# Opening of an attention and FFN kernel: order of key splits, layer norm, query weights and first queries

## What is computed

```python
x = x + _L0_xattn_ref(_layernorm(x), ctx, ctx, proj_q, bias_q, proj_k, bias_k, proj_v, bias_v, w_out)
x = x + _L0_ffn_ref(_layernorm(x), w_gate, w_up, w_down)
...
q = jnp.einsum('bnd,hdk->bhnk', query, proj_q) + bias_q      # k and v in the same way, from ctx
attn = jax.nn.softmax(jnp.einsum('bhqk,bhnk->bhqn', q, k) / scale, axis=-1)
hid = heads of attn @ v;  result = hid @ w_out.T
...
h = silu(fp4_linear(x, w_gate)) * fp4_linear(x, w_up);  result = fp4_linear(h, w_down)
```

## Time and profile before

| | us |
|---|---|
| timed runs | 394.61, 397.33, 397.7 (median 397.33) |
| the profiled execution | 398.0, span 396.1 |
| PE busy | 333.8 (84% of the span) |
| DVE busy | 310.3 (78%) |
| ACT busy | 266.7 (67%) |
| POOL busy | 257.6 (65%) |

### The profile page before, as it was taken

How to read it: one execution, slowest core, us unless ns; L and a number is a source line. 1 busy time by engine, 2 the same in 40 slices (tenths; PEclk the granted TensorE clock), 3 DMA queues, 4 the chain that set the end, 5 groups by cost and what they waited for, 6 DMA issues and landing times.

```text
span 396.1 us, 9486 instructions
## 1 busy us (share of the span) xinstructions
PE 333.8 (84%) x3571; PEld 254.4 (64%) x3571; DVE 310.3 (78%) x629; ACT 266.7 (67%) x634; POOL 257.6 (65%) x254
## 2 busy tenths in 40 slices
PE   1777669998799989989895877898878999999976
PEld 1455448776587767767674666676656767677854
DVE  1979845766777778687899877679999999998692
ACT  3566687987899999999986689734352553542431
POOL 7272244786579898998985586738844667767510
PEclk9989958999999999999999899999998999999999
DMA  7990535797599899997995698831000000000001
GB/s 209 321 357 2 102 66 107 120 148 136 96 133 174 151 171 180 156 186 146 187 168 96 120 159 131 133 63 26 15 14 15 13 15 27 14 13 29 16 26 40
DMA packets 131710, 42.42 MB, mean 107 GB/s; under 512 B 123788, under 2 KB 129616, under 8 KB 131665
## 3 DMA queue, kind: packets, MB, share of 16 engines
q1 hardware_dynamic: 131665, 41.82, 55.3%
HBM read 8.78 MB, written 2.10 MB: 27 GB/s over the span
## 4 chain that ended last, share of the span: by engine, by line
DVE 42%; PE 32%; ACT 11%; issue 8%; POOL 4%; DMA 2%; SPq 0%; ACTq 0%; DVEq 0%
PE ps L572 5%; PE ps L493 5%; PE ps L495 5%; PE ps L494 5%; DVE arena L1191 4%; ACT arena L853 4%; DVE negmax L1110 4%; PE ps L629 4%; DVE arena L1141 3%; DVE arena L1193 3%; DVE arena L1314 3%; DVE arena L1280 2%; POOL arena L1387 2%; DVE arena L1126 2%; DVE arena L1145 2%
## 5 line engine op out<-in xcount | busy, mean ns | idle before, releaser
L1387 POOL TENSOR_TENSOR arena<-arena 128x640 f16<-128x640 f32 x64 | 93.0, 1453 | 58.0 <-ACT arena L863 57.6
L853 ACT ACTIVATE arena<-ps,negmax 128x154 f32<-128x154 f32 x256 | 78.6, 398 | 15.6 <-DVE negmax L1110 15.3
L572 PE MATMUL ps<-v_h,pT 128*128 128x132 f16 (+1 forms) x640 | 52.8, 214 | 17.2 <-DVE q_odd L1102 8.8
L1110 DVE TENSOR_REDUCE negmax<-ps 128x4 f32<-128x616 f32 x64 | 50.9, 795 | 20.1 <-PE ps L629 19.8
L572 PEld LDWEIGHTS ps<-v_h,pT 128*128 128x128 f16 x640 | 38.9, 100 | 24.6 <-issue 22.9
L1392 POOL TENSOR_TENSOR arena<-arena 128x256 f16<-128x256 f32 x64 | 46.5, 728 | 8.0 <-ACT arena L870 8.0
L863 ACT ACTIVATE arena<-arena 128x640 f16<-128x640 f32 x64 | 47.4, 741 | 1.2
L493 PE MATMUL ps<-arena 128*128 128x256 f16 (+1 forms) x144 | 41.6, 289 | 7.4 <-DVE arena L1013 5.9
L493 PE MATMUL ps<-arena,xnT_even 128*128 128x352 f16 x128 | 40.1, 313 | 4.8 <-DVE xnT_even L1202 4.1
L494 PE MATMUL ps<-arena 128*128 128x256 f16 (+1 forms) x144 | 41.3, 287 | 0.0
L495 PE MATMUL ps<-arena 128*128 128x256 f16 (+1 forms) x144 | 41.2, 286 | 0.0
(11 more groups left out here) (163 smaller groups left out, 943.7 us busy)
## 6 DMA issues: line engine op xcount, KB each, us to landing
out_dram<-arena SPq DMA_DIRECT2D x16, 128.0 KB, 1.7
pT<-arena SPq DMA_TRANSPOSE x70, 4.2
xs<-in_x_dram SPq DMA_DIRECT2D x2, 512.0 KB, 7.3
arena<-in_L_xattn_w_out_dram SPq DMA_DIRECT2D x1, 1024.0 KB, 11.8
xs<-in_x_dram SPq DMA_DIRECT2D x2, 384.0 KB, 6.7
wffn<-in_L_ffn_w_down_dram SPq DMA_DIRECT2D x1, 704.0 KB, 9.3
wffn<-in_L_ffn_w_gate_dram SPq DMA_DIRECT2D x1, 640.0 KB, 7.7
wffn<-in_L_ffn_w_up_dram SPq DMA_DIRECT2D x1, 640.0 KB, 8.2
```

The source lines that it names most:

```text
L572: last = pe.matmul(o[:, h0 * HB:h1 * HB], pT[:, n % RING_P, part * CHUNKS + c], v[:, b, j, at[0]:at[-1] + 1].rearrange("p m k -> p (m k)") ...
L853: last = act.activation(prob[:, j, k * LP:k * LP + L], ps[:, 2 * (j % 2) + k % 2, (k // 2) * L:(k // 2 + 1) * L], ACT.Exp, bias=negmax[:, ...
L1110: dve.tensor_reduce(negmax[:, s, 4 * j:4 * j + 4].rearrange("p (k u) -> p u k", k=2), v, AX.X, ALU.max, negate=True).then_inc(max_done, 1)
L1387: pool.tensor_tensor(part_of(j, 1), prob[:, j], part_of(j, 0), ALU.subtract).then_inc(p_low, 1)
```

## The change

- The first two loads of x bring the rows of steps 0 and 1, not of step 0 alone; proj_v is loaded ahead of the rest of x.
- PE does 12 transposes of the identity into a bank that nothing reads (`WARM`) behind those of ctx. Keys 0 to 2 are then computed first on chunk 0, then on chunk 1 of their inputs (`KEYS_FIRST`), each as soon as that chunk's weights are split (`wk_split`); keys 3 and 4 follow (`KEYS_NEXT`), then the turning of step 0's rows, keys 5 to 7, and the first two query tasks. The other two stand in slots 0 and 1.
- The low half of the key weights goes from DVE to POOL, ahead of the query weights'; bias_v's comes behind those.
- ACT splits the query weights ahead of all key copies, normalises step 1's rows ahead of slot 0, and splits the value weights behind the first two query copies.
- DVE runs one layer norm of 4 columns for steps 0 and 1 ahead of slot 0; statistics of steps 2 to 7 come in slots 0 to 2 and their layer norm (12 columns) in slots 3 and 4.
- Step 1's rows are turned in slot 0 (before: 5), its queries stand in slots 2 to 5 (6 to 9), values of batch 0 in slots 1 to 4 (0 to 3), output weights in slots 5 to 8 (4, 4, 5, 6), step 2's rows in slot 6 (5).

```diff
+WARM = 12
+KEYS_FIRST = 3
+KEYS_NEXT = 5
...
+        wk_split = sem("wk_split")
...
-            return n if b == 0 else 11 + 2 * n
+            return 1 + n if b == 0 else 11 + 2 * n
...
-            return (4, 4, 5, 6)[n]
+            return 5 + n
...
-            return 3 if i == 1 else 5 if i == 2 else 8 * (i - 1) - 6
+            return 6 if i == 2 else 8 * (i - 1) - 6
...
-            return 6 + p // 2 if i == 1 else 8 * (i - 1) + (2 if i == 2 else 1) + p
+            return p // 2 - 2 if i == 0 else 2 + p // 2 if i == 1 else 8 * (i - 1) + (2 if i == 2 else 1) + p
...
-            out = [t for i in range(1, STEPS) for t in query_tasks(i) if query_at(i, t[2]) == n]
-            out += [("x", 1)] if n == 5 else []
+            out = [t for i in range(STEPS) for t in query_tasks(i) if query_at(i, t[2]) == n]
+            out += [("x", 1)] if n == 0 else []
...
-        TASKS = [("x", 0)] + query_tasks(0)
+        FIRST_QUERIES = [t for t in query_tasks(0) if query_at(0, t[2]) < 0]
+        TASKS = [("x", 0)] + FIRST_QUERIES
...
+            def pairs_of_rows(b):
+                return x[b].rearrange("(i v p) d -> v p i d", v=2, p=P)
...
-                sp.dma_start(xs[:, v, 0], x[0, rows_of(0, v)]).then_inc(ld_x0, 16)
+                sp.dma_start(xs[:, v, 0:2], pairs_of_rows(0)[v, :, 0:2]).then_inc(ld_x0, 16)
...
+            load_proj("v", proj_v, ld_v)
...
-                pairs = x[b].rearrange("(i v p) d -> v p i d", v=2, p=P)
-                first = 1 if b == 0 else 0
+                first = 2 if b == 0 else 0
...
-                    sp.dma_start(xs[:, v, b * STEPS // B + first:(b + 1) * STEPS // B], pairs[v, :, first:]).then_inc(ld_x, 16)
-            load_proj("v", proj_v, ld_v)
+                    sp.dma_start(xs[:, v, b * STEPS // B + first:(b + 1) * STEPS // B],
+                                 pairs_of_rows(b)[v, :, first:]).then_inc(ld_x, 16)
...
+            for _ in range(WARM):
+                pe.transpose(ps[:, PROJ_BANK, 0:P], ident[:, :], ident[:, :])
+            def keys(p, c):
+                return three(bank(J_K + p)[:, 0:B * L], wk_h[:, c, p * P:(p + 1) * P], wk_l[:, c, p * P:(p + 1) * P],
+                             cT_h[:, c, :, 0:L], cT_l[:, c, :, 0:L], c == 0, c == KC - 1)
...
-            pe.wait_ge(w_low, 1)
-            for p in range(PAIRS):
+            for c in range(KC):
+                pe.wait_ge(wk_split, c + 1)
+                for p in range(KEYS_FIRST):
+                    if c == 0: free(J_K + p)
+                    last = keys(p, c)
+                    if c == KC - 1: last.then_inc(job_mm, 1)
+            def keys_of(p):
...
-                    last = three(bank(J_K + p)[:, 0:B * L], wk_h[:, c, p * P:(p + 1) * P],
-                                 wk_l[:, c, p * P:(p + 1) * P], cT_h[:, c, :, 0:L], cT_l[:, c, :, 0:L],
-                                 c == 0, c == KC - 1)
+                    last = keys(p, c)
...
-                        pe.wait_ge(w_low, 3)
+                        pe.wait_ge(w_low, 2)
...
+            for p in range(KEYS_FIRST, KEYS_NEXT):
+                keys_of(p)
...
-            pe.wait_ge(w_low, 2)
-            for t in query_tasks(0):
+            for p in range(KEYS_NEXT, PAIRS):
+                keys_of(p)
+            pe.wait_ge(w_low, 1)
+            for t in FIRST_QUERIES:
...
+            act.wait_ge(ld_q, 16)
+            split_proj("q", wq_h, 1.0)
...
-            for p in range(PAIRS):
+            for p in range(KEYS_NEXT):
...
-                if p == 3:
-                    act.wait_ge(ld_q, 16)
-                    split_proj("q", wq_h, 1.0)
...
+            for p in range(KEYS_NEXT, PAIRS):
+                keys_out(p)
...
-                if n == 3: act.wait_ge(ln_step, 2 * LN_ROWS)
-                for r in range(1, STEPS):
+                if n == rows_at(2): act.wait_ge(ln_step, 2 * LN_ROWS)
+                for r in range(2, STEPS):
...
-                        if r >= 2: rows_high(r)
+                        rows_high(r)
...
-            act.wait_ge(w_scaled, 1)
-            split_part("v", wv_h, 1.0, 0)
-            high(("q", 0, 0))
-            split_part("v", wv_h, 1.0, 1)
-            for t in query_tasks(0)[1:]:
+            act.wait_ge(ln_step, LN_ROWS)
+            rows_normal(1)
+            for t in FIRST_QUERIES:
...
+            act.wait_ge(w_scaled, 1)
+            split_proj("v", wv_h, 1.0)
...
-            dve.wait_ge(ld_k, 16)
-            for c in range(KC):
-                dve.wait_ge(w_high, c + 1)
-                last = dve.scalar_tensor_tensor(heads_of(wk_l, c), by_chunk("k")[:, c], 1.0, heads_of(wk_h, c),
-                                                ALU.mult, ALU.subtract)
-            last.then_inc(w_low, 1)
...
+            def stats_of(i):
+                for b in range(B):
+                    row_stats(b, i).then_inc(stats_done, 1)
...
-            for b in range(B):
-                row_stats(b, 0).then_inc(stats_done, 1)
-            dve.wait_ge(stats_done, B)
-            layernorm(0, 1, 0)
+            stats_of(0)
+            stats_of(1)
+            dve.wait_ge(stats_done, 2 * B)
+            layernorm(0, 2, 0)
...
-            for p in range(PAIRS):
+            def keys_low(p):
...
+            for p in range(KEYS_NEXT):
+                keys_low(p)
...
-            def stats_of(i):
-                for b in range(B):
-                    row_stats(b, i).then_inc(stats_done, 1)
+            for p in range(KEYS_NEXT, PAIRS):
+                keys_low(p)
...
+                    dve.wait_ge(ld_x, 32 * B)
+                    stats_of(2)
+                    stats_of(3)
+                if n == 1:
+                    stats_of(4)
...
+                if n == 2:
...
-                if n == 1:
+                if n == 3:
...
-                    layernorm(1, STEPS, LN_ROWS, [0, 1])
-                if n == 2: layernorm(1, STEPS, LN_ROWS, [2, 3, 4])
+                    layernorm(2, STEPS, LN_ROWS, [0, 1])
+                if n == 4: layernorm(2, STEPS, LN_ROWS, [2, 3, 4])
...
-            dve.wait_ge(ld_x, 32 * B)
-            stats_of(1)
-            stats_of(2)
-            for t in query_tasks(0)[0:2]:
-                low(t)
-            stats_of(3)
-            stats_of(4)
-            for t in query_tasks(0)[2:]:
+            for t in FIRST_QUERIES:
...
+            def proj_low(n, name, high, low, c):
+                pool.wait_ge(w_high, KC * n + c + 1)
+                return pool.tensor_tensor(heads_of(low, c), by_chunk(name)[:, c], heads_of(high, c), ALU.subtract)
+            for c in range(KC):
+                proj_low(0, "k", wk_h, wk_l, c).then_inc(wk_split, 1)
+            proj_low(1, "q", wq_h, wq_l, 0)
+            proj_low(1, "q", wq_h, wq_l, 1).then_inc(w_low, 1)
...
-            for n, name, high, low in ((1, "q", wq_h, wq_l), (2, "v", wv_h, wv_l)):
-                for c in range(KC):
-                    pool.wait_ge(w_high, KC * n + c + 1)
-                    last = pool.tensor_tensor(heads_of(low, c), by_chunk(name)[:, c], heads_of(high, c), ALU.subtract)
-                last.then_inc(w_low, 1)
+            proj_low(2, "v", wv_h, wv_l, 0)
+            proj_low(2, "v", wv_h, wv_l, 1).then_inc(w_low, 1)
```

More of the change, by code:

```diff
@@ L935, in slot @@
                 if n == 63: magnitude_x(1)
+            act.wait_ge(ln_step, LN_ROWS)
+            rows_normal(1)
+            for t in FIRST_QUERIES:
+                high(t)
             act.wait_ge(w_scaled, 1)
-            split_part("v", wv_h, 1.0, 0)
-            high(("q", 0, 0))
-            split_part("v", wv_h, 1.0, 1)
-            for t in query_tasks(0)[1:]:
-                high(t)
+            split_proj("v", wv_h, 1.0)
             act.activation(unused[:, 0:1], biasT[:, 0:1], ACT.Exp)
```

## The result

The changed kernel took **403.06 us** (median of 4, 402.28 to 405.09) against 397.51 for the kernel before beside it: a ratio of 1.0164, interval 1.0130 to 1.0198. Run once more later it took 401.64, a ratio of 1.0111 (1.0052 to 1.0170). So it is slower, by 1.6% and 1.1% in the two sets, above the predicted 400.0, just beyond the upper end of the range (403.0), and on the side that had a chance of 0.25. The profiled execution took 405.09 us (span 403.3), that of before 398.0 (span 396.1): 7.2 us of span to find. It is the slowest of the four; the medians lie 5.5 us apart, and 4.8 in the later set.

The account below looks back on a forecast made before the run. PE was taken as full from 62.4 us on, held up before by waits and half clock; terms 0.8 + 2.8 - 1.4 - 11.4 + 4.5 + 5.0 + 1.6 = +1.9 on 398.0 gave 400.0 us, range 392.5 to 403.0.

Parts of the forecast that it names:

- Opening: Before slot 0: POOL's subtractions hold up DVE's layer norm, normalised rows at 24.2, score 0 at 32.8 against 32.04: +0.8 us.
- rival 1: Opening, faster: POOL does not hold the layer norm up, score 0 at about 25.5; 393 us; chance 0.22.
- Two queries behind score 0: Start of the slots: two query tasks of 1.41 us each now stand behind score 0 on PE: +2.8 us.
- the waits and the half clock of slots 4 to 7: Slots 4 to 7: four PE waits, 6.9 us, and the half clock, 4.5 us, go: -11.4 us.
- the wait at slot 1: Slot 1: PE idles 2.4 us for copies of step 1's rows and value weights, plus 2.1 in clock: +4.5 us.
- (d): Slot 10: PE waits for the transposing transfer of step 2's rows, normalised in slot 6, not 5: +1.6 us.
- (c): Slots 5 to 9: output weights' copies through ACT and DVE leave PE waits of 0.2 to 1.6, together +5.0 us.
- Rival 2: Slower: PE drops to the lower clock in more stretches, slot 2 or slots 5 to 7, +2 to +4: 403; chance 0.18.
- Rival 3: No change: (c) and (d) are smaller, output weights' copies hide behind the heads, 3 us go: 397; chance 0.10.

Follow-up runs that it names:

- experiment 1: Changed kernel with POOL's low-half query-weight subtractions waiting until the first layer norm has ended: 401.61 us, ratio 1.0120.
- experiment 2: Changed kernel with POOL's query subtractions waiting until step 0's rows are normalised: 395.03 us, ratio 0.9953.
- experiment 6: Changed kernel with the query task of slot 1 in PSUM bank 6 in place of 7: 400.01 us, ratio 1.0070.
- experiment 3: Changed kernel with step 2's rows normalised in slot 5 again instead of slot 6: 396.15 us, ratio 0.9988.
- experiment 4: Changed kernel without the twelve throwaway transposes: 400.16 us, ratio 1.0090.
- experiment 5: Changed kernel with the twelve throwaway transposes moved from ahead of the keys to behind key 4: 402.80 us, ratio 1.0146.
- experiment 9: Kernel before the change with twelve throwaway transposes added ahead of its keys: 395.72 us, ratio 0.9967.

## Why the prediction was right and where it failed

**Opening (+0.8 forecast).** The mechanism held, down to the number of links that slip in: one at each change of POOL's instruction, as the earlier trace rows had it. Rows at 23.6 against 24.2 forecast; score 0 at 32.11 against 32.8, thus +0.1 to before. The exclusive lock of the Trainium skill, "SBUF — State Buffer", section "Who interferes with whom", agrees with the four links that ended with POOL's instructions; that POOL's next one always wins, which the prediction added to it, would put the rows at 24.8 and is further off. Experiments 1 and 2 show by taking the overlap away that this hold cost about 6 us (experiment 2: 6.3 at slot 0, 6.0 at slot 16): rival 1 fell, but its price for a free chain, 6.9 us below the forecast, was near.

**The slots up to 10.** Two queries behind score 0, the waits and the half clock of slots 4 to 7 given back, the wait at slot 1 (35.05 to 37.52, forecast 35.7 to 38.1), the copies of output weights: together with the opening, my terms without (d) gave +0.3 at slot 10; the trace has -0.5. That this is so near is in part luck. The opening came 0.7 cheaper and the term of slot 1 was 2.9, not 4.5 (experiment 6), which alone would make -2.0; so the other terms cost 1.5 more than forecast. Which, was not measured; the waits of (c) in the list are 3.1 for wot_l.

**The step that failed is the size of (d)**, +1.6, measured 4.5. Its path was right: PE stands at slot 10 for this transfer, and one slot earlier takes the loss away (experiment 3). Issue was at 69.30, as forecast (69.2). But PE was there at 71.0, not 72.5; the transfer landed at 74.9, not 74.1; and the term had nothing for the clock, which was at the lower level behind the wait, from 75.4 to 78.8. So the wait is 3.9, 2.3 more than forecast: 1.5 for the early PE and 0.8 for the landing. Without the packet (experiment 4) the wait is 2.3, the clock stays up, and slots 10 to 11 lose 1.2 in place of 4.5: of these 3.3 us 1.7 are wait; the rest, by difference, is the clock. So the throwaway transposes, which I had at nothing but for the clock, cost that much by where they put the packet (experiments 4 and 5). In experiments 1, 2 and 6 the issue came forward with the slots ahead, and slot 16 kept their gain.

The 4.9 that I took for the landing is the median of three transfers in the trace of before. They took 3.1, 4.9 and 5.5 us, the latter two with a 16 KB packet in them, the one in question without. So the packet's part was in my number by luck, and the larger miss is the margin: before, the transfer was issued at 60.9 and PE came to it at 71.7, 10.8 us later; in the changed kernel at 69.3 and 71.0, 1.7 us later. The rows stand one slot later, and slot 5 itself is 7.4 us later while slot 10 is not.

**Two clock falls** at 113 and 239, 3.0 us together in the first profile, were not in the sum. At 112.07 PE resumes after a wait of 2.4 us for v_l that the kernel before has too, at 108.05, without a fall behind it (timelines of PE, first the changed kernel, then before):

```profile
112.07 0.40 PE L591 MATMUL ps<-v_h,pT 128*128 128x66 f16 x5 [2.38 <-DVE v_l L1086]
```

```profile
108.05 0.40 PE L572 MATMUL ps<-v_h,pT 128*128 128x66 f16 x5 [2.37 <-DVE v_l L1068]
```

The changed kernel and all its versions show a fall there and take 9.4 us from slot 18 to 20; the kernel before and experiment 9 show none and take 7.8. Why is open. The fall at 239 is in the changed kernel's first profile and in that of experiment 6 alone. Rival 2 gave 403 by such stretches, but at slot 2 and slots 5 to 7, where they did not come, so that its number is met by luck: up to 80 us the changed kernel ran at the lower level for 13.6 us (20.8 to 27.6, 37.8 to 41.2, 75.4 to 78.8), the kernel before for 17.1 (24.8 to 28.2, and 48.7 to 62.4).

The account: +1.9 forecast, +2.9 for (d), -0.8 up to slot 10, +3.0 for the two falls, 0.2 at the end, makes 7.2. Rival 3, smaller (c) and (d), fell with (d).

## What to carry to other kernels

When a change moves slots, count for every later transfer the time from its issue to the instruction that needs it, before and after (10.8 and 1.7 us here); its slot is the cheapest thing to move (one number here, worth 1.2 to 1.8% by the ratios). Keep GpSimd's large SBUF subtractions out of the stretch in which VectorE runs a short chain that others wait for, its last instruction included. Look at what else DMA carries beside a transfer that you price, instruction packets too: a median over transfers with and without one hides two groups.

## What the runs showed of the hardware

- A 16 KB packet of the instruction queue in a transposing transfer: landed in 5.3 to 5.6 us with it, in 3.9 without, at the same place. Over all profiles 34 transfers with one landed in 4.8 to 5.8 us, 38 without in 3.1 to 4.1. Twelve idle transposes more or fewer moved the packet, by 4.4 us, over 60 us behind the place of the edit.
- Two normalising instructions on VectorE (128x256 fp32, one SBUF tensor and two columns of scalars) took 4.56 us beside two subtractions of GpSimd, 0.87 without.
- A wait of TensorE of 2.4 us (for v_l, behind slot 18) was followed by the lower clock in every version of the changed kernel and not in the two profiles of the kernel before.
